# Third layer of a four-layer convolution kernel: neighbour sums through DRAM, blocks in pairs, roots in groups of six blocks

## The reference, cut to what matters

```python
xp = jnp.pad(x, ((0, 0), (0, 0), (pad, pad), (pad, pad)))
wins = jnp.stack([xp[:, :, i:i + H, j:j + W] for i in range(K) for j in range(K)])
pw = wins[..., None] ** jnp.arange(DEG_P, dtype=x.dtype)
P = jnp.einsum('pbchwi,fcpi->fpbchw', pw, A)
Q = 1.0 + jnp.abs(jnp.einsum('pbchwi,fcpi->fpbchw', pw[..., 1:1 + DEG_Q], Bc))
out = jnp.sum(P / Q, axis=(1, 3))
```

## Time and profile before

| What | us |
|---|---|
| median of 3 runs (lowest, highest) | 12135.7 (12120.45, 12162.18) |
| the profiled execution, its own time | 12114.81 |
| span of the profile | 12112.6 |
| third layer: first and last multiply (L1309) start | 6023.3, 11135.7 |
| busy in the span: PE, DVE, ACT, POOL | 9570.5, 8958.4, 7397.5, 5088.7 |

### The profile page before, as it was taken

How to read it: one execution, slowest core, us unless ns; L and a number is a source line. 1 busy time by engine, 2 the same in 40 slices (tenths; PEclk the granted TensorE clock), 3 DMA queues, 4 the chain that set the end, 5 groups by cost and what they waited for, 6 DMA issues and landing times. The chain is left out here.

```text
span 12112.6 us, 205123 instructions
## 1 busy us (share of the span) xinstructions
PE 9570.5 (79%) x53055; PEld 4412.5 (36%) x53055; DVE 8958.4 (74%) x10913; ACT 7397.5 (61%) x10963; POOL 5088.7 (42%) x2442
## 2 busy tenths in 40 slices
PE   0788578857886788640199999999999999997599
PEld 0566456645664566510022222222222222222233
DVE  1778487847784787637488888888888888887677
ACT  0455345534553455324288888888888888886354
POOL 0233133312321233100166666666666666665243
PEclk9899789977997799875599999999999999999799
DMA  2000100010000000004311111111111111112544
GB/s 86 1 0 0 28 8 0 0 29 7 0 0 21 15 0 0 37 28 143 98 29 29 29 27 25 28 29 29 29 29 29 29 29 27 28 26 54 130 115 100
DMA packets 227136, 410.60 MB, mean 34 GB/s; under 512 B 28784, under 2 KB 163024, under 8 KB 212336
## 3 DMA queue, kind: packets, MB, share of 16 engines
q1 hardware_dynamic: 226150, 399.26, 12.9%
HBM read 283.44 MB, written 115.70 MB: 33 GB/s over the span
## 5 line engine op out<-in xcount | busy, mean ns | idle before, releaser
L1194 POOL TENSOR_TENSOR l_a<-l_a 128x1018 f32<-128x1018 f32 x1851 | 3453.3, 1883 | 1687.8 <-ACT l_a L1339 1673.0
L1309 DVE TENSOR_TENSOR l_r<-l_pps,l_a 128x509 f32<-128x509 f32 x4755 | 2989.0, 677 | 46.0 <-PE l_pps L1208 28.1
L1333 ACT ACTIVATE l_a<-l_qps 128x509 f32<-128x509 f32 x3705 | 2155.3, 596 | 818.4 <-PE l_qps L1208 566.0
L1339 ACT ACTIVATE l_a<-l_a 128x1018 f32<-128x1018 f32 x2380 | 2504.0, 1052 | 40.3 <-issue 40.3
L1208 PE MATMUL l_qps<-l_mv,l_wst 123*128 123x509 bf16 x4235 | 1644.6, 388 | 170.1 <-ACT l_a L1333 50.0
L1208 PE MATMUL l_pps<-l_mv,l_wst 123*128 123x509 bf16 x4228 | 1624.4, 384 | 63.6 <-DVE l_r L1309 60.9
L652 POOL TENSOR_TENSOR a_pr<-a_pr 128x768 f32<-128x768 f32 x384 | 898.4, 2340 | 1639.1 <-DVE a_pr L567 1624.0
L681 ACT ACTIVATE a_g<-a_fps 128x512 f32<-128x512 f32 x1152 | 680.4, 597 | 998.7 <-PE a_fps L434 997.3
L434 PE MATMUL a_fps<-a_hbt,a_wfc 96*128 96x512 f32 x2304 | 1222.2, 666 | 70.2 <-ACT a_g L681 70.2
L452 POOL TENSOR_TENSOR a_pr<-a_qkv 128x768 f32<-128x768 f32 x128 | 386.6, 3039 | 2089.3 <-ACT a_qkv L694 2089.3
L1297 DVE TENSOR_SCALAR l_a<-l_qps 128x509 int32<-128x509 int32 x1058 | 724.5, 685 | 688.2 <-PE l_qps L1208 677.6
(11 more groups left out here) (162 smaller groups left out, 12030.2 us busy)
## 6 DMA issues: line engine op xcount, KB each, us to landing
l_mv<-pw SPq DMA_DIRECT2D x1608, 79.5 KB
l_gx<-g SPq DMA_DIRECT2D x66, 1040.0 KB
pw<-pw_hi SPq DMA_DIRECT2D x165, 127.2 KB
pw<-pw_mid SPq DMA_DIRECT2D x165, 127.2 KB
pw<-pw_lo SPq DMA_DIRECT2D x165, 127.2 KB
a_tb<-g SPq DMA_DIRECT2D x16, 1031.9 KB
l_x<-x SPq DMA_DIRECT2D x16, 1024.0 KB, 12.1
l_gs<-g SPq DMA_DIRECT2D x33, 260.0 KB
```

The source lines that it names most:

```text
L1194: g.tensor_tensor(a, a, a, ALU.mult).then_inc(sq_p, 2)
L1309: v.tensor_tensor(R[:, m % R_RING, :], pps[:, m % P_BANKS, 0:SUB], A[:, m % A_RING, :], ALU.mult).then_inc(mul_done, 1)
L1333: s_.activation(A[:, s % A_RING, :], qps[:, s % Q_BANKS, 0:SUB], ACT.Abs).then_inc(abs_a, 1)
L1339: s_.activation(a, a, ACT.Abs_reciprocal_sqrt, bias=1.0).then_inc(root_done, 2)
```

## The change

The unit of a step becomes a pair of blocks (nine pairs a subtile). q of a pair goes to two of four banks and is made absolute by one instruction of 1018 columns; in a cycle of 18 pairs (two subtiles) DVE takes pairs 1, 4, 7, 11 and 15. The root takes three pairs at once (3054 columns), a step after the last of them. POOL squares all but pair 5 of the cycle, which DVE does. P still has three banks, and the lags are now P 6, multiply 7 in steps of a pair. The sums come in two bursts of eight matmuls a subtile, after pairs 3 and 7. The centre quotients of a supertile are kept in `RC` and summed by one burst of eight matmuls, four row groups at once. The sums `S` of a supertile are written to a DRAM tensor `planes`; eight DMAs read them back, each 16 rows at its tap's offset, into `SH`; a supertile later four matmuls (`gather`) add the 128 rows up, and DVE adds the centre (`add`). All of these sums share one PSUM bank, `aux`. Before the loop three DMAs, each waited for, write zeros to the edges of `planes`.

```diff
-STEPS = SUBS * NBLK
-Q_BANKS, P_BANKS, A_RING, R_RING = 2, 3, 18, 9
-assert NBLK % Q_BANKS == 0 and NBLK % P_BANKS == 0 and NBLK % A_RING == 0 and NBLK % R_RING == 0
-
-ABS_DVE = {3, 7, 11, 15}
-SQ_DVE = {4, 5, 12, 13}
-
-LAG_ROOT, LAG_SQ, LAG_P, LAG_MUL, LAG_SUM, LAG_COPY = 3, 4, 7, 8, 10, 11
-
-
-SHIFT_FROM, SHIFT_EVERY = 2 * NBLK - 10, 5
-COPY_OUT = SHIFT_FROM + 7 * SHIFT_EVERY + 3
+STEPS = SUBS * NPAIR2
+Q_PAIRS, P_BANKS, A_PAIRS, GROUP = 2, 3, 12, 3
+assert NPAIR2 % GROUP == 0 and A_PAIRS % GROUP == 0 and STEPS % A_PAIRS == 0 and STEPS % Q_PAIRS == 0 and 2 * STEPS % P_BANKS == 0
+
+CYCLE = 2 * NPAIR2
+ABS_DVE = {1, 4, 7, 11, 15}
+SQ_DVE = {5}
+LAG_ROOT, LAG_SQ, LAG_P, LAG_MUL, LAG_SUM, LAG_COPY, LAG_LATE = 1, 6, 6, 7, 9, 10, 11
 LOADED = SLOTS * NSUB * NBLK
+LEAD = 2 * SUP
+FRONT = SUP + MARGIN
+SHIFTED = len(AROUND) * 16
...
+                edges = ((0, SUP), (SUP, FRONT), (FRONT + LINE, FRONT + LINE + MARGIN))
+                for k, (lo, hi) in enumerate(edges):
+                    sp.dma_start(planes[:, lo:hi], S[:, 0, 0:hi - lo]).then_inc(s_stored, 16)
+                    sp.wait_ge(s_stored, 16 * (k + 1))
...
+                def store_planes(g, k):
+                    sp.wait_ge(s_copied, g * NSUB + NSUB)
+                    sp.dma_start(planes[:, bass.ds(g * SUP + FRONT, SUP)], S[:, k, :]).then_inc(s_stored, 16)
+
+                def load_shifted(v, k, planes_stored):
+
+                    sp.wait_ge(s_stored, planes_stored)
+                    sp.wait_ge(o_made, v + 2)
+                    for n, tap in enumerate(AROUND):
+                        at = v * SUP + (FRONT + OFFS[tap])
+                        sp.dma_start(SH[C * n:C * n + C, k, :], planes[C * n:C * n + C, bass.ds(at, SUP)]).then_inc(sh_in[k], 16)
+
+                def store(v, bank):
+                    sp.wait_ge(o_added, v + 3)
                     for j in range(NSUB):
-                        sp.dma_start(out2[:, bass.ds(n * SUP + j * SUB, SUB)], O[32 * j:32 * j + C, bank, :]).then_inc(stored[bank], 16)
+                        sp.dma_start(out2[:, bass.ds(v * SUP + (LEAD + j * SUB), SUB)], O[32 * j:32 * j + C, bank, :]).then_inc(stored[bank], 16)
...
+                        g = it * BODY + u
+                        store_planes(g, u % 2)
+                        load_supertile(g + SLOTS, u)
+                        load_shifted(g - 1, (u + 1) % 2, it * (BODY * 16) + 16 * (u + 1) + 48)
+                        store(g - 2, u % 2)
...
+                g.memset(S[:, 0, :], 0.0).then_inc(cleared, 1)
                 g.memset(mv[:], 1.0).then_inc(cleared, 1)
-                g.memset(S[:], 0.0).then_inc(cleared, 1)
+                g.memset(SH[:], 0.0).then_inc(cleared, 1)
+                g.memset(CS[:], 0.0).then_inc(cleared, 1)
                 g.memset(O[:], 0.0).then_inc(cleared, 1)
-                pool.wait_ge(cleared, 3)
...
                     m = s - LAG_SQ
-                    if m >= 0 and m % 2 == 0 and m % NBLK in sq_pool:
-                        a = A[:, m % A_RING:m % A_RING + 2, :]
-                        pool.wait_ge(root_done, it * STEPS + m + 2)
-                        g.tensor_tensor(a, a, a, ALU.mult).then_inc(sq_p, 2)
+                    if m >= 0 and m % CYCLE in sq_pool:
+                        a = pair_of(A, m)
+                        pool.wait_ge(root_done, it * STEPS + m // GROUP * GROUP + GROUP)
+                        g.tensor_tensor(a, a, a, ALU.mult).then_inc(sq_p, 1)
...
+                def gather(k):
                     for j in range(NSUB):
-                        a = 0
-                        while a < SUB:
-                            src = j * SUB + OFFS[AROUND[k]] + a
-                            where, src = src // SUP, src % SUP
-                            n = min(SUB - a, SUP - src)
-                            last = t.matmul(ops[32 * j:32 * j + 32, bank, a:a + n], pick[:, k, :],
-                                            S[:, (slot + where) % SLOTS, src:src + n],
-                                            start=False, stop=k == len(AROUND) - 1, skip_group_check=True)
-                            a += n
-                    if k == len(AROUND) - 1:
-                        last.then_inc(o_made, 1)
+                        last = t.matmul(aux[32 * j:32 * j + 32, 0:SUB], pick[:], SH[:, k, j * SUB:(j + 1) * SUB],
+                                        start=True, stop=True, skip_group_check=True)
+                    last.then_inc(o_made, 1)
...
 
-                    if s >= Q_BANKS:
-                        wait_abs(pe, it, s - Q_BANKS)
-                    product(1, s, qps[:, s % Q_BANKS, 0:SUB]).then_inc(q_made, 1)
+                    if s >= Q_PAIRS:
+                        wait_abs(pe, it, s - Q_PAIRS)
+                    for h in range(2):
+                        last = product(1, sub, 2 * n + h, qps[:, 2 * (s % Q_PAIRS) + h, 0:SUB])
+                    last.then_inc(q_made, 1)
                     m = s - LAG_P
                     if m >= 0:
-
-                        pe.wait_ge(mul_done, it * STEPS + m - P_BANKS + 1 + A_RING)
-                        product(0, m, pps[:, m % P_BANKS, 0:SUB]).then_inc(p_made, 1)
+                        sub, n = divmod(m, NPAIR2)
+                        for h in range(2):
+                            pe.wait_ge(mul_done, it * (2 * STEPS) + 2 * m + h - P_BANKS + 1 + 2 * A_PAIRS)
+                            product(0, sub, 2 * n + h, pps[:, (2 * m + h) % P_BANKS, 0:SUB]).then_inc(p_made, 1)
                     m = s - LAG_SUM
                     if m < 0:
                         return
-                    sub, n = divmod(m, NBLK)
+                    sub, n = divmod(m, NPAIR2)
                     u, j = divmod(sub, NSUB)
-                    if n < NPAIRED and n % NPP == NPP - 1:
-                        pe.wait_ge(mul_done, it * STEPS + m + 1 + A_RING)
-                        if n == NPP - 1:
-
-                            pe.wait_ge(s_copied, it * SUBS + sub + 1)
-                        for pp in range(NPP):
-                            last = t.matmul(sps[32 * pp:32 * pp + 32, 0:SUB], sums[:, 0, :],
-                                            R[:, (m - NPP + 1 + pp) % R_RING, :], start=n == NPP - 1,
-                                            stop=n == NPAIRED - 1, skip_group_check=True)
-                        last.then_inc(summed, NPP)
-                    if n >= NPAIRED:
-                        pe.wait_ge(mul_done, it * STEPS + m + 1 + A_RING)
-                        if n == NPAIRED and j == 0:
-
-                            pe.wait_ge(o_copied, it * BODY + u + 1)
-                        t.matmul(ops[32 * j:32 * j + 32, u % 2, 0:SUB], sums[:, 1, :], R[:, m % R_RING, :],
-                                 start=n == NPAIRED, stop=False, skip_group_check=True).then_inc(summed, 1)
-
-
-                    k, odd = divmod(m % (NBLK * NSUB) - SHIFT_FROM, SHIFT_EVERY)
-                    if 0 <= k < len(AROUND) and not odd:
-                        if k == 0:
-                            pe.wait_ge(s_copied, it * SUBS + u * NSUB + 1 + 1)
-                        shifted_sum(k, (u + 1) % 2, (u - 1) % SLOTS)
+                    if n in (3, 7):
+                        if n == 3:
+                            if j == 0:
+                                pe.wait_ge(c_copied, it * BODY + u + 3)
+                            elif j == 3:
+                                pe.wait_ge(o_added, it * BODY + u + 1)
+                            else:
+                                pe.wait_ge(s_copied, it * SUBS + sub)
+                        pe.wait_ge(mul_done, it * (2 * STEPS) + 2 * (m + 1) + 2 * A_PAIRS)
+                        for b in range(2 * n - 6, 2 * n + 2):
+                            pp = b % NPP
+                            last = t.matmul(aux[32 * pp:32 * pp + 32, 0:SUB], sums[:, 0, :], R[:, b, :], start=b < NPP,
+                                            stop=b >= NPAIRED - NPP, skip_group_check=True)
+                        last.then_inc(summed, 1)
+                    m -= 1
+                    if m < 0:
+                        return
+                    sub, n = divmod(m, NPAIR2)
+                    u, j = divmod(sub, NSUB)
+                    if n == CPAIR and j == 2:
+                        pe.wait_ge(s_copied, it * SUBS + sub + 1)
+                        pe.wait_ge(sh_in[u % 2], (it * (BODY // 2) + (u + 1) // 2 + (u + 1) % 2) * SHIFTED)
+                        gather(u % 2)
+                    if n == CPAIR and j == 3:
+                        pe.wait_ge(s_copied, it * SUBS + sub + 1)
+                        pe.wait_ge(mul_done, it * (2 * STEPS) + 2 * (m + 1) + 2 * A_PAIRS)
+                        for h in range(2):
+                            for i in range(NSUB):
+                                last = t.matmul(aux[32 * i:32 * i + 32, 0:SUB], sums[:, 1, :], RC[:, i, h, :],
+                                                start=h == 0, stop=h == 1, skip_group_check=True)
```

(125 more changed lines are left out.)

104 lines of the change are left out of this document (49 added, 55 removed).

## The result

The changed kernel takes 12731.7 us (median, 12726.8 to 12742.1), the kernel before 12128.1 in the same comparison: ratio 1.0496, 95% interval 1.0470 to 1.0521, 604 us slower. I forecast slower, 12500, range 11980 to 12800. The direction and the place are right; of the 604 us my forecast had 365 (12500 over 12135), so nearly two fifths of the loss were missing from it.

A forecast was written before the change was run, and what follows sets the result against it. Waits between engines, none of them full, were taken to bound the kernel. 12115 us profiled, plus 249 for the chain, 29 for the ends and 99 for the clock, made 12492; with 21 for the median, 12500, range 11980 to 12800.

The forecast's parts named there:

- Nobody is full; the time is set by waits: Layer before the change: no engine fills the 77.4 us of a supertile; engines wait for one another.
- the first rival: Whole loop: turn-taking and bursts hide, POOL's 62.6 us a supertile sets the pace, 11170 us; chance 0.20.
- In a step with DVE's absolute value PE and DVE work in turn: Five steps per cycle of 18 pairs: each takes 2.81 us, 1.63 more than a plain step.
- The chain is 81.1 us: Per supertile: two cycles of 38.7 us plus gather, centre burst, add and waits; layer 5361 against 5112, +249.
- The burst ahead of q of pair 4 counts in full, and the others in part: Bursts of eight per cycle: 1.96 us in step 3, 1.5 in step 12, 1.94 each in steps 7 and 16.
- The square of pair 5 lies in the chain, 1.5: DVE's one square per cycle adds 1.5 us to the chain.
- The round trip is hidden: DRAM write and reads of the sums: covered by the supertile in between, with 60 us of room.
- Ends +29: Before and after the loop: zero writes, memsets, longer fill and final stores add 29 us, between 15 and 50.
- The clock, 1.5 us a supertile, +99: PE's clock falls 4 us behind each of two long holes a supertile; 1.5 us taken, 99 on the layer.
- For DVE's squares the rows show less than a full block: Shared ports of DVE and POOL: 1208 to 1926 ns taken, not a full block's up to 3.1 us.
- Bursts hidden by half: PE's bursts, rival: 3.7 of 7.3 us per cycle hidden, 73.7 us a supertile, 11,900 to 12,150; chance 0.10.
- The clock falls in most of the ten holes: PE's idle stretches, rival: 4 us more per supertile than the forecast took, 12760 us; chance 0.13.

The follow-up runs named there:

- The last experiments: Changed kernel, DVE multiplying before its absolute values, all squares on POOL: with two absolute values a cycle on DVE 11777.5 us, with six 11648.9.
- the filled holes: Changed kernel with PE repeating a product, result unchanged, where it would only wait in steps with DVE's absolute value: 12425.1 us, ratio 1.0256.
- the reorder: Changed kernel with DVE's absolute value moved from the head of its step to behind the multiplies: 11819.4 us, ratio 0.9745.
- the last but one experiment: Changed kernel, DVE multiplying first, six absolute values a cycle and the square of pair 5 on DVE, other squares on POOL: 12014.7 us, ratio 0.9928.

## Why the prediction came out as it did

- *Nobody is full; the time is set by waits.* Right. PE, DVE and ACT were busy less than before (711, 446 and 461 us), and the layer grew. POOL's work rose, though, from 52 to 62.6 us a supertile by my own sum, so "every engine sum falls", which I gave for the first rival, was wrong. The last experiments show the engine limit only once the waits are gone: 69.9 us with POOL at 95%.
- *In a step with DVE's absolute value PE and DVE work in turn.* Right, and shown by the reverse: the order alone is worth 912 us, with what it gives back of the clock.
- *The chain is 81.1 us.* Measured 82.2 with the clock at 1.00. It isn't the square: its turn is 1.79 where it meets POOL's (8011.70 to 8013.49) and 1.12 where it doesn't (8052.27 to 8053.39), about one of each a supertile, so 2.9 for the 3.0 of the sum. What makes up the 1.1 is open. The break-even I gave, 38 us a cycle, was a slip: with the 3.7 us outside the cycles it is 36.9.
- *The burst ahead of q of pair 4 counts in full, and the others in part.* A burst of eight measured 1.94 against 1.96. How much of each burst lies in the chain was not tested alone.
- *The square of pair 5 lies in the chain, 1.5.* Partly: taking it out gives 2.0 us a supertile in place of 3.0, at a nearly full clock.
- *The round trip is hidden.* Right in the loop, no wait for it. At the very end two gathers wait 14.9 us for the reads, which is in the next item.
- *Ends +29.* Right: 28. From the layer's first memset to its first multiply it takes 63.9 us for 53.0 (5954.26 to 6018.1 now, 5970.32 to 6023.3 before), and from the last multiply to the end of the span 993.6 for 976.9. The 11.5 us outside the loop are these 28 less the 16 by which the layers before, which the change doesn't touch, ended earlier in this execution.
- *The clock, 1.5 us a supertile, +99.* This is the step that failed, by size: 4.4 us a supertile, 296 us in the loop by the filled holes. I gave two long holes a fall of 4 us each, 8 us at the low level, priced that at 2.5 and took 1.5 of it. The trace has 2.5 falls a supertile, most of them by the long holes as I had it, but they last 5.2 us on average, 13.0 in all. With 13.0 in place of 8 and the full price of my own sum (25/81) it would have been 4.0. The mechanism was right. In all, 249 + 29 + 99 should have been about 305 + 28 + 296, and the layers before took 16 off. As to the rule I had set beside it (the Trainium skill, "TensorE: Matmul & The Clock Gate", A second HAM failure mode: psum-queue depth-cycling), the trace agrees: the clock goes back and forth between its two levels in a loop over PSUM banks, 0.92 on average, and 1.00 with the holes filled.
- *For DVE's squares the rows show less than a full block.* The reading was wrong; see below. It cost the sum nothing, as the item on the chain shows.
- *Rivals.* Engine-bound was the case only after the reorder. Bursts hidden by half and a late round trip didn't occur. "The clock falls in most of the ten holes" (0.13) forecast 12760, and 12732 was measured, but its mechanism is not what happened: the clock fell 2.5 times in ten holes, mostly at the long ones. That its number was the closest is luck.
- *What would show it.* The signs came, with two off: a pair step took 2.40 us (86.6/36), not 2.2 to 2.35, and DVE idled 28 us a supertile, not 20. Part of both is the clock.

## What to carry to other kernels

Doubling the unit of a software pipeline while a ring of buffers keeps its size halves the steps that the ring covers: look which instruction of the same step now hangs on which, and put the one that another engine waits for ahead of the one that itself waits. An engine sum that falls is no forecast when nobody was full. Holes in PE's work have a second price in its clock, so a relieved PE can be slower: here a fall lasted longer on average than the hole that it belonged to (5.2 us in the changed kernel), and holes that did little beside longer ones cost as much once those were gone.

## What the hardware showed that I had not expected

PE work without use made the kernel 307 us faster: the granted clock went from 0.92 to 1.00 in the middle of the layer with the holes of 1.79, 2.92 and 3.57 us filled.

A square on DVE and one on POOL exclude each other for a whole instruction. The timeline of POOL where the two meet:

```profile
8012.45 2.86 POOL L1231 TENSOR_TENSOR l_a<-l_a 128x1018 f32<-128x1018 f32 x1
```

DVE's square started at 8011.70, while POOL's first was running to about 8012.49, and ended at 8013.56: 1.86 us for 1.21 of work. POOL's next, started at 8012.45, took 2.86 for 1.88 of work. In the last but one experiment, six absolute values and a square on DVE, DVE's square takes up to 2775 ns, 1.57 us more than alone:

```profile
L1345 DVE TENSOR_TENSOR l_a<-l_a x132: 1208/1211/2775, 6048.2 to 10997.6; 128x1018 f32<-128x1018 f32 x132
```

The rows of the kernel before show the same. There POOL's squares never stretched (1879 to 1887) and DVE's did (to 1926); I took that for less than a full block. A pair from its timeline:

```profile
7009.12 1.57 DVE L1303 TENSOR_TENSOR l_a<-l_a 128x1018 f32<-128x1018 f32 x1 [0.44 <-ACT l_a L1339]
```

```profile
7007.73 1.88 POOL L1194 TENSOR_TENSOR l_a<-l_a 128x1018 f32<-128x1018 f32 x1 [0.52 <-ACT l_a L1339]
```

POOL's ended at 7009.61 and DVE's at 7010.69, 1.08 us later. Of DVE's 529 squares there 389 began while one of POOL's had over 0.2 us to run, and every one of the 389 ended 1.07 to 1.08 us after POOL's, however early it had begun; in no case did POOL begin during one of DVE's. So DVE did its whole square behind POOL's, and the stretch was short only because POOL was near its end when DVE came. In the changed kernel 122 of POOL's squares began during one of DVE's, and each of them ended 1.74 us after it. To tell a full block from a part of one, compare the two ends, not the lengths. The Trainium skill's sentence in "SBUF — State Buffer" (SBUF: two separate sides), which I had set aside, agrees with these rows. DVE's multiplies, with one input from PSUM, stay at 669 to 693 ns whatever POOL does.
